# Attention over two branches: squares moved behind two v copies, and the product with the inverted row sums moved from GpSimd to VectorE

## What is computed

```python
v = group_norm(x)                                 # 32 groups
g = relu(mean(v) @ w1 + b1) @ w2 + b2             # a gate per channel
m = (sigmoid(g) > 0.5)
hyp = logmap0(mhsa(expmap0(v * m), hdn weights))
euc = mhsa(v * (1 - m), eu weights)
out = x + hyp + euc
# mhsa: qkv = t @ w_qkv + b; softmax(q k^T / 8) v for 8 heads of 64; @ w_o + b_o
```

## Time and profile before

| | |
|---|---|
| median of 3 runs | 3930.74 us (3926.16 to 3931.89) |
| profiled execution | 3919.98 us |
| its span | 3918.1 us |
| TensorE busy | 3832.2 us, 98% |
| VectorE busy | 2651.1 us, 68% |
| ScalarE busy | 1918.0 us, 49% |
| GpSimd busy | 2662.5 us, 68% |

### The profile page before, as it was taken

The page is one execution under the profiler, slowest core; times in us unless marked ns, Lnnn a source line. Parts: engine busy times, 40 slices in busy tenths (PEclk is TensorE's granted clock), DMA queues, the critical chain, the costliest instruction groups (busy, mean ns, idle before and its releaser), DMA issues.

```text
span 3918.1 us, 57425 instructions
## 1 busy us (share of the span) xinstructions
PE 3832.2 (98%) x21164; PEld 2396.1 (61%) x21164; DVE 2651.1 (68%) x3576; ACT 1918.0 (49%) x3489; POOL 2662.5 (68%) x1300
## 2 busy tenths in 40 slices
PE   5999999999999999999999999999999999999999
PEld 3656565565665656566565665656556565565665
DVE  6675856758667585776857668576685757847566
ACT  4454534545345453554535555354453545536444
POOL 4583866838668486774867658675586856868468
PEclk9999999999999999999999999999999999999999
DMA  8312122121321213112141121411213112121101
GB/s 285 103 44 97 33 97 81 44 97 33 100 82 53 91 33 118 66 52 85 36 147 44 49 81 33 145 49 49 76 48 131 49 49 76 54 97 44 65 12 65
DMA packets 137556, 293.14 MB, mean 75 GB/s; under 512 B 16705, under 2 KB 28993, under 8 KB 127297
## 3 DMA queue, kind: packets, MB, share of 16 engines
q1 hardware_dynamic: 137280, 289.47, 21.7%
HBM read 239.09 MB, written 50.33 MB: 74 GB/s over the span
## 4 chain that ended last, share of the span: by engine, by line
PE 91%; DVE 5%; issue 1%; POOL 1%; DMA 1%; ACT 0%; SPq 0%; ACTq 0%; POOLq 0%; DVEq 0%
PE aux_ps L1360 31%; PE score_ps L1445 22%; PE acc_ps L1459 22%; PE aux_ps L1409 8%; PE score_ps L1360 4%; PE aux_ps L1473 3%; DVE mxp L1197 2%; DVE neg_max L1220 1%; POOL sums L690 1%; DMA xin<-in_x_dram 0%; DVE sc L977 0%; DVE ss L1061 0%; DVE xin L1097 0%; DMA w_split<-w_o 0%; DVE den L1281 0%
## 5 line engine op out<-in xcount | busy, mean ns | idle before, releaser
L690 POOL TENSOR_TENSOR sums<-sums,probs 128x1024 f32<-128x1024 f32 x765 | 1834.2, 2398 | 751.8 <-ACT probs L871 697.4
L1197 DVE TENSOR_REDUCE mxp<-aux_ps 128x2 f32<-128x1024 f32 x1014 | 1240.2, 1223 | 907.8 <-PE aux_ps L1409 897.8
L871 ACT ACTIVATE probs<-score_ps 128x512 f32<-128x512 f32 x2048 | 1060.0, 603 | 997.2 <-PE score_ps L1445 725.3
L1459 PE MATMUL acc_ps<-probs,v_y 128*64 128x512 f32 x4096 | 955.3, 599 | 0.5 <-ACT probs L871 0.5
L1360 PE MATMUL aux_ps<-xs,w_qk 128*128 128x512 f32 x2976 | 753.3, 401 | 0.0
L1360 PEld LDWEIGHTS aux_ps<-xs,w_qk 128*128 128x128 f32 x2976 | 537.8, 188 | 195.0 <-issue 89.3
L1459 PEld LDWEIGHTS acc_ps<-probs,v_y 128*64 128x64 f32 x4096 | 270.3, 136 | 529.0 <-issue 390.0
L690 POOL TENSOR_TENSOR sums<-probs 128x1024 f32<-128x1024 f32 x128 | 306.1, 2391 | 335.6 <-ACT probs L871 335.5
L1409 PE MATMUL aux_ps<-k_hi,q_hi 64*128 64x512 f32 x2028 | 460.5, 447 | 17.5 <-DVE mxp L1197 14.6
L1281 DVE RECIPROCAL den<-den 128x256 f32<-128x256 f32 (+1 forms) x240 | 444.0, 1850 | 14.8 <-ACT den L882 13.4
L1445 PE MATMUL score_ps<-q_hi,k_hi 64*128 64x512 f32 x2048 | 409.2, 393 | 0.4 <-ACT q_max L811 0.4
(11 more groups left out here) (139 smaller groups left out, 3195.2 us busy)
## 6 DMA issues: line engine op xcount, KB each, us to landing
w_qk<-w_split SPq DMA_DIRECT2D x124, 512.0 KB, 4.2
xin<-in_x_dram SPq DMA_DIRECT2D x232, 256.0 KB, 3.4
w_o<-w_split SPq DMA_DIRECT2D x32, 1024.0 KB, 7.8
w_v<-w_split SPq DMA_DIRECT2D x30, 1024.0 KB, 7.0
v_y<-in_x_dram SPq DMA_DIRECT2D x72, 256.0 KB, 3.1
y<-v_y SPq DMA_DIRECT2D x64, 256.0 KB, 2.0
xin<-y SPq DMA_DIRECT2D x64, 256.0 KB, 3.0
out_dram<-v_y SPq DMA_DIRECT2D x64, 256.0 KB, 6.5
```

The source lines that it names most:

```text
L690: pool.tensor_tensor(sums[h][:, :], a, probs[:, g % SLOTS_P, :], ALU.add).then_inc(c_sum[h].sem, 1)
L871: act.activation(probs[:, n % SLOTS_P, token_half(u % 2)], score_ps[:, u % SCORE_BANKS, :], ACT.Exp, scale=SCALE).then_inc(c_exp.sem, 1)
L1197: dve.tensor_reduce(mxp[:, :, n, h], ps, AX.X, ALU.max).then_inc(c_free["D"].sem, 1)
L1459: last = nc.tensor.matmul(acc_ps[head(j), :], v_y[:, m, head(2 * p + j)], probs[:, n % SLOTS_P, token_half(j)], start=(m == 0), stop=(m == ...
```

## The change

Two things move. First, `operand_step` of ScalarE, which in half 1 makes the squares: in the batches with v tiles (0 and 2) it comes behind the second of the four v copies, no longer ahead of all of them; in other batches it stays. Second, `mult` leaves GpSimd's order and enters VectorE's: in batch 4ph + 9 behind the second maximum (and the reciprocals, of which there are none in those batches) and ahead of the tail and the transposes; for phase 6 behind the last reciprocals of batch 31, ahead of the `o_lo` of phase 5; for phase 7 right behind its reciprocal.

```diff
@@ gpsimd
-                    def mult(ph):
-
-                        n = 8 * t + ph
-                        pool.wait_ge(c_rec.sem, c_rec.at(i, RECIP_PARTS * (n + 1)))
-                        pool.wait_ge(c_raw.sem, c_raw.at(i, n + 1))
-                        pool.tensor_tensor(o_raw[:, ph % 2, :], o_raw[:, ph % 2, :], den[:, ph % 2, :], ALU.mult).then_inc(c_on.sem, 1)
-
...
-                        if closing(i, t) and b == BATCHES - 2:
-                            mult(2 * PAIRS - 2)
                         for g in (2 * b, 2 * b + 1):
-                            if g == TILES - 1 and not closing(i, t):
-                                mult(2 * PAIRS - 2)
                             if g % NT and not (closing(i, t) and g >= TILES - NT + 1 + LAST_SUMMED):
                                 probs_sum(g // NT, g % NT)
-                        if phase_at(b, MULT) is not None:
-                            mult(phase_at(b, MULT))
                     for k in range(8):
-                        if k == 3:
-                            mult(2 * PAIRS - 1)
                         if t:
                             y_sum(k)
@@ scalar
                             if f[0] == "v":
                                 v_out(f[1])
+                                if f[1] % 4 == 1:
+
+                                    operand_step(i, t, b)
...
-                        operand_step(i, t, b)
+                        if 2 * b >= NT or b % 2:
+                            operand_step(i, t, b)
@@ vector
+                    def mult(ph):
+
+                        n = 8 * t + ph
+                        dve.wait_ge(c_rec.sem, c_rec.at(i, RECIP_PARTS * (n + 1)))
+                        dve.wait_ge(c_raw.sem, c_raw.at(i, n + 1))
+                        dve.tensor_tensor(o_raw[:, ph % 2, :], o_raw[:, ph % 2, :], den[:, ph % 2, :], ALU.mult).then_inc(c_on.sem, 1)
+
...
                         for ph, parts in recips(b):
                             recip(ph, parts)
+                        if phase_at(b, MULT) is not None:
+                            mult(phase_at(b, MULT))
+                        if b == BATCHES - 1:
+                            mult(2 * PAIRS - 2)
                         if t:
                             operand_tail(i, t, b)
...
                     recip(2 * PAIRS - 1, (0, RECIP_PARTS))
+                    mult(2 * PAIRS - 1)
```

## The result

The changed kernel takes 4034.28 us in the median of six runs (4021.16 to 4043.68), the kernel before 3928.51 us (3922.29 to 3931.89) beside it: a ratio of 1.0268, 95% interval 1.0248 to 1.0288. It is slower by 106 us; 4044 were predicted, with 3950 to 4085 as the range. The profiled execution of after is the longest of its six, 4043.68 us with a span of 4041.9, so the two traces differ by 123.8 us, 18 more than the medians.

What follows compares the result with a forecast made beforehand. TensorE, busy 98% of the span at full clock, was taken as the bound. Squares -22, halves 0 +24, halves 1 +98, last half +2, ends +11 gave +113: 3920 to 4033, plus 10.8 for the median 4044 us; range 3950 to 4085.

Steps and rivals of the forecast that it cites:

- Squares: Batch 2 of half 1: v copies pass ahead of squares 4 and 5, removing 7 TensorE stalls; -22 us.
- Halves 0: Eight halves with six plain gaps each: VectorE's product waits for GpSimd's sum, 48 x 0.50 = 24 us.
- Halves 1 with their ends: Seven halves 1: late VectorE instructions wait for GpSimd's sums, 98 us; ends where ScalarE's accumulator drain is late, 1.4 each.
- I take 14, the middle: Loss per image in half 1, taken between 9.6 and 18.7 us; 7 x 14 = 98 us.
- Ends of halves: Product of phase 6 delays ScalarE's accumulator drain: 0.1 us per half 0, 1.4 per half 1, together 11 us.
- Last half: Last half of the last image: four plain gaps on VectorE, 2 us.
- Clock: Granted clock read as full in all 40 slices, with nothing to give; no term in the sum.
- The signs named beforehand: No v-copy waits; product 1.5 us or more; maxima waits over 80 us, mostly behind batches 9 and 21; small instructions over 1.
- A: Each gap costs TensorE 0.50 us, instructions behind keep clear of GpSimd: 3959 us; chance 0.17.
- B: Product doesn't wait, costs 0.68 us and fits VectorE's idle time; faster, 3919 us; chance 0.10.
- C: Moving the squares brings no gain because the wait for the chunk moves to tile 6: 4066 us; chance 0.05.
- D: Full cascades of VectorE waits in half 1, 131 us: 4077 us and a little above; chance 0.08.

Runs made afterwards that it cites:

- the short sums: Changed kernel with GpSimd's sums over half of the columns, the other half left out: 3897.84 us, ratio 0.9924.
- 0.77 us without a wait: Changed kernel with a reciprocal of 100 columns of den on VectorE in place of the product, which is left out: 3929.09 us, ratio 1.0007.
- the squares alone: Kernel before with only ScalarE's squares moved behind two of the four v copies, product still on GpSimd: 3891.19 us, ratio 0.9911; again 3891.59 us, 0.9920.
- the product between the maxima: Changed kernel with VectorE's product one batch later, right behind the first maximum of batch 4ph + 10: 4015.71 us, ratio 1.0232.

## Why the prediction was right, point by point
In the terms of the sum, against the difference of the two traces (113 us predicted, 124 measured):

- **Squares, -22 predicted, -28.6 measured.** The mechanism was right, all seven stalls are gone and square 5 now waits 0.3 us for its chunk while tile 6 is made. The size was too small: I took the idle time of the waits for the whole price. The stretch lengthened by some 0.3 us more each time: the matmul ahead of the stall is drawn to 0.39 us where a successor follows after 0.23, and the first one behind it is followed after 0.33. And it lengthened by another 1.6 to 2.9 us on the two images where the granted clock fell. The 0.3 us of the chunk, on ScalarE:

```profile
359.75 0.82 ACT L743 ACTIVATE xin<-xin,shift,keep 128x512 f32<-128x512 f32 x1 [0.32 <-DMA xin<-in_x_dram]
```

- **Halves 0, 24 predicted, 19.3 measured.** 0.42 us a gap in place of 0.50. The price had been read from one other batch of half 1.
- **Halves 1 with their ends, 98 + 10 predicted, 134 measured** (19.2 us an image). The number is at the upper end of the range, 18.7 (18.9 with 2.2 for both of the last two), and not at "I take 14, the middle". But what failed in size is for the most part the clock, which the sum has at nothing: all of the 23 us of clock that the trace of after lacks lie in these halves. Taken off in full, they leave about 111 us, beside the 108 predicted. Batches 9 to 12: 6.2 of 3.7 to 8.2. Batches 14 and 15: 2.4 of 0.5 to 2.8. Batch 17: 0.4 of 0.5. Batch 21: 3.2 of 0.9 to 3.0; the second product sat out the second sum, at 2.86 us. This is 3.8 to 4.0 us on the four images on which the clock fell behind it, and 2.3 on the other three. Batch 29: 3.6 of 2.0 to 2.2, but 2.3 to 2.6 on five images, and 7.1 and 6.1 on two, behind waits of 3.29 and 3.30 us after which the clock fell too. Batch 25: 3.4 of 2.0 to 2.2, and here it is not the clock: 2.0 us on three images, 4.3 and 4.4 on three, 5.1 on one. On the first image two of the three small instructions of batch 26 wait for a sum, 5.04 us from 516.20 on, where the first sum begins at the same 516.20; on the second image only one does, 2.38 us at 1015.21, 0.30 us behind the sum of 1014.91.
- **Ends of halves, 11 predicted.** Nearly nothing: TensorE's waits for that low part are 0.8 us in all in the trace of after. The product there did take 2.51 us (at 300.08), as long as a sum and more, but there was more slack behind it than I had counted.
- **Last half, 2 predicted, 0.4 measured.**
- **Clock, not in the sum.** I read the 9s of the slices as full; a 9 says 90% or more. The clock had something to give: the trace of before lacks 5 us of it behind the stalls for the v copies, which are a part of the 28.6, and most unprofiled runs lack more. And it had more to lose: 23 us behind the new stalls.

The errors go both ways, and that the total comes so near is in part luck. Squares (6.6 us), halves 0 (5) and the last half (1.6) were forecast too dear, the halves 1 with their ends 26 us too cheap; 1.4 us ahead of the first half are in no term. The sum is 11 us low against the traces and 9.7 us high against the median, since the 10.8 us between trace and median of before turned round: the profiled run of after is 9.4 us above its median. Of the waits of TensorE inside the image loop I had called two the only ones; there are three more, of 0.3, 0.5 and 0.8 us, which change nothing.

**The signs named beforehand.** The waits for the v copies are gone, the product takes 1.76 us in the mean, and the waits for the maxima are 114 us. Two signs came out weaker. Batches 9 and 21 have 53 of the 114 us behind them, about half and not most; 13, 25 and 29 have 44. And of the six small instructions of batches 10 and 11 three are above 1 us in the mean of the seven images (1.89, 2.42 and 1.79); the others are at 0.29, 0.27 and 0.88.

**The rivals.** A (0.5 us a gap and nothing behind it, 3959) fell with the cascades: six gaps at 0.42 us are 2.5 of the 19.2 us of an image. B (the product fits, faster) is what the short sums show: with the wait gone the same change gives 0.9924. It was wrong here because the first sum is still running; and its 1.5 us an image behind batches 9 and 21 is little, since 0.77 us without a wait already cost 5.7 us behind batch 9. C fell with the squares alone. D (full cascades, 131 us for the halves 1) has the number, 134, but by the clock and not by its mechanism: in the first cascade shown above the third instruction is free.

## What to carry to other kernels
Before an elementwise instruction is moved from GpSimd to VectorE, look what GpSimd is executing at the moment at which it would start. Here a product with two SBUF inputs (0.69 us when free, 1.84 in the median) and line 974 with one (0.23 and 2.42 us) waited until the running GpSimd instruction was over; a reciprocal (766 to 779 ns in all 128) did not. Then look at VectorE's instructions behind it, since those that were just ahead of the next GpSimd instruction, by a few tens of nanoseconds, can each lose a whole one of them once they are late. And where TensorE is busy 98% of the time and does not wait for GpSimd, such a move had nothing to give; the gain was in an order of ScalarE's that cost nothing.

## What the runs showed of the hardware
The granted clock falls after some of the longer stalls. Two stretches of the changed kernel (columns as above):

```profile
2035.00:2040.00 5.00, 2.52 (x11) 1.00 0.27 103
2040.00:2045.00 5.00, 4.19 (x20) 0.51 0.00 0
...
3540.00:3545.00 5.00, 1.70 (x11) 1.00 0.01 3
3545.00:3550.00 5.00, 5.00 (x26) 0.66 0.01 3
```

0.51 in a stretch of 5 us means that nearly all of it ran at 1.2 GHz in place of 2.4. It comes right behind a stall of TensorE, of 3.29 us in the first case and 3.30 in the second. Not every stall is followed by it: behind one of 2.92 us that ended at 491.60 the clock stayed at 1.00, and behind one of 2.92 us that ended at 3482.47 it fell. What decides between them was not found. Summed over stretches of 5 us with under 0.95, the trace of before lacks 5 us of clock in 3 stretches, that of after 23 us in 20, that with the product between the maxima 34 us in 24, that of the squares alone none. That is up to 18 of the 124 us. In batch 22 of the changed kernel it can be seen image by image: 4.2 us on the four images where the clock fell there, 2.7 on the other three. With the order of the two engines in batch 26 it is a reason why a half 1 costs 11.5 us on one image and 20.4 on another. It explains less of the spread of the runs of the changed kernel, 4021 to 4044 us: all six have a mean clock of 0.993 or 0.994, and a thousandth is 4 us. The rest of that spread stays open.
